# Int8 cross attention: scores read 1024 columns at a time, one weighing per turn, six of eight casts on ScalarE, values held twice

## The reference, cut to what matters

```python
def _fq_sym(x, axis):          # queries, keys, values
    s = jnp.maximum(jnp.max(jnp.abs(x), axis=axis, keepdims=True) / 127.0, 1e-08)
    q = jnp.clip(jnp.round(x / s), -127.0, 127.0) * s
def _fq_unsigned(x, axis):     # probabilities
    s = jnp.maximum(jnp.max(x, axis=axis, keepdims=True) / 255.0, 1e-08)
    q = jnp.clip(jnp.round(x / s), 0.0, 255.0) * s
...
scores = q @ k.T * scale ; p = softmax(scores) ; out = fq_unsigned(p) @ v
```

## Time and profile before

| | |
|---|---|
| median of 3 runs | 2608.09 us (2602.43 to 2608.8) |
| profiled execution | 2601.35 us, span 2599.5 us |
| busy in the span | TensorE 2309.8 us (89%), VectorE 1796.6 (69%), ScalarE 1244.8 (48%), GpSimd 588.7 (23%) |
| int8 stage | from 1522 us to 2139 us of the span |

### The profile page before, as it was taken

How to read it: one execution, slowest core, us unless ns; L and a number is a source line. 1 busy time by engine, 2 the same in 40 slices (tenths; PEclk the granted TensorE clock), 3 DMA queues, 4 the chain that set the end, 5 groups by cost and what they waited for, 6 DMA issues and landing times. The chain is left out here.

```text
span 2599.5 us, 32403 instructions
## 1 busy us (share of the span) xinstructions
PE 2309.8 (89%) x11664; PEld 1576.3 (61%) x11664; DVE 1796.6 (69%) x3528; ACT 1244.8 (48%) x2202; POOL 588.7 (23%) x435
## 2 busy tenths in 40 slices
PE   3779999999999999877897988888888779899998
PEld 2557666666666665555774455545555437677776
DVE  7855777767777779786776976777767763554444
ACT  4443465666565666533443124676767853211111
POOL 7710033333333243430000004222141300000000
PEclk9889999999999999998998999999989879899999
DMA  3331100000000000005444000000000004556662
GB/s 130 114 138 37 37 17 29 9 29 25 13 29 17 29 9 13 1 16 203 162 170 171 0 21 10 1 10 1 10 1 1 21 27 188 188 205 232 234 229 70
DMA packets 47067, 184.89 MB, mean 71 GB/s; under 512 B 6272, under 2 KB 11136, under 8 KB 36672
## 3 DMA queue, kind: packets, MB, share of 16 engines
q1 hardware_dynamic: 46912, 182.86, 19.5%
HBM read 173.93 MB, written 8.91 MB: 70 GB/s over the span
## 5 line engine op out<-in xcount | busy, mean ns | idle before, releaser
L403 PE MATMUL wide_a<-wide_w,ctxT 128*128 128x256 f32 (+1 forms) x2048 | 437.8, 367 | 2.8 <-POOL wide_eps L372 2.8
L403 PEld LDWEIGHTS wide_a<-wide_w,ctxT 128*128 128x128 f32 x2048 | 368.2, 191 | 76.8 <-issue 35.7
L385 POOL TENSOR_TENSOR wide_sums<-wide_sums,wide_s 128x512 f32<-128x512 f32 x224 | 301.9, 1348 | 458.3 <-ACT wide_s L533 445.1
L428 PE MATMUL wide_scores<-wide_q,wide_keysT 128*128 128x512 f32 x512 | 238.4, 604 | 10.8 <-ACT wide_s L529 10.8
L1702 ACT ACTIVATE int_prob<-int_a,int_shift,int_qscale 128x512 uint8<-128x512 f32 x256 | 198.8, 781 | 102.3 <-PE int_a L1551 101.8
L438 PE MATMUL wide_o<-wide_s,wide_values 128*128 128x512 f32 x512 | 232.5, 597 | 3.5 <-ACT wide_s L533 3.5
L529 ACT COPY wide_s<-wide_scores 128x512 f32<-128x512 f32 x256 | 148.5, 586 | 180.0 <-PE wide_scores L428 168.6
L1827 DVE TENSOR_REDUCE int_peaks<-int_a 128x1 f32<-128x512 f32 x256 | 169.3, 684 | 52.9 <-PE int_a L1551 50.9
L1551 PE MATMUL int_a<-int_keys,int_qrows 96*128 96x512 bf16 x512 | 166.5, 408 | 42.6 <-DVE int_peaks L1827 37.3
L428 PEld LDWEIGHTS wide_scores<-wide_q,wide_keysT 128*128 128x128 f32 x512 | 87.9, 189 | 147.0 <-ACT wide_s L529 86.0
L591 DVE TENSOR_TENSOR wide_top<-wide_top,wide_s 128x512 f32<-128x512 f32 x240 | 165.5, 690 | 15.4 <-ACT wide_s L529 9.6
(11 more groups left out here) (426 smaller groups left out, 4283.3 us busy)
## 6 DMA issues: line engine op xcount, KB each, us to landing
moe_gate_up<-hbm_m_gu SPq DMA_DIRECT2D x34, 1408.0 KB, 6.1
moe_down<-hbm_m_down_a SPq DMA_DIRECT2D x34, 512.0 KB, 7.0
causal_wqkv<-hbm_wqkv SPq DMA_DIRECT2D x8, 1536.0 KB, 6.8
ctxT<-hbm_ctxT SPq DMA_DIRECT2D x4, 2048.0 KB, 15.3
oproj_raw<-hbm_wproj SPq DMA_DIRECT2D x8, 1024.0 KB, 5.3
ctxT_again<-hbm_ctxT SPq DMA_DIRECT2D x4, 2048.0 KB, 14.7
moe_down<-hbm_m_down_b SPq DMA_DIRECT2D x34, 192.0 KB, 7.2
wide_unit<-hbm_ffn_units SPq DMA_DIRECT2D x24, 256.0 KB, 2.6
```

The source lines that it names most:

```text
L385: ins = pool.tensor_tensor(sums[0][:, :], before, part[:, j, :], ALU.add)
L403: mm = pe.matmul(a[h][:, j, cols], ctxT[:, kc, t * P:(t + 1) * P], w[g % 2][:, kc, cols], start=(kc == 0), stop=(kc == KC - 1))
L428: pe.matmul(sp_[j % 2][:, :], keysT[:, j, :], q[:, :], start=True, stop=True).then_inc(s_s, 1)
```

## The change

- The four PSUM tiles of 512 columns become two tiles `wide` of 1024 columns. A step `first` or `second` is now two matmuls into one of them, one reduction or one exponential of 1024 columns. `a_free(n)` waits for the reader of tile n-2, so "second" always uses tile 0 and "first" tile 1 (each kind has one tile).
- Order: "first" of a step stands behind the first half of the step's product rather than next to "second". Every turn is followed by one weighing, that of two turns before, across heads too; "summed" (copy of int_sums on VectorE) is a step of its own; "finish" comes two turns after the chunk's last weighing. The four "value turned" are spread over four steps and begin earlier, for which `values` and `pscale` exist twice.
- VectorE casts j = 0 and 4 of a head (in the last chunk j = 0, 2, 4, 6), ScalarE the others; before, VectorE cast the even j (in the last chunk six of eight).
- The program's reserve for DMA descriptors (`dynamic_dma_scratch_size`) goes from 8192 to 2048, which makes room in SBUF.

```diff
-        values = st.sb("values", [P, NCT, P], BF16)
+        values = [st.sb(f"values{i}", [P, NCT, P], BF16) for i in range(2)]
-        a = [st.ps(f"a{i}", [P, 512]) for i in range(4)]
+        wide = [st.ps(f"a{i}", [P, 1024]) for i in range(2)]
+        a = [wide[i // 2][:, i % 2 * 512:(i % 2 + 1) * 512] for i in range(4)]
...
         def cast_on_vector(h, j):
-            if h // HC + 1 == CC:
-                return j % 4 != 3
-            return j % 2 == 0 and not (j % 4 == 2 and h % HC == HC - 1)
+            return j % (2 if h // HC + 1 == CC else 4) == 0
...
                 def a_free(n):
-                    if n >= 4:
-                        who, seen = done_a[n - 4]
+                    if n >= 2:
+                        who, seen = done_a[n - 2]
...
-                    pe.matmul(a[n % 4][:, :], qrows[0:3 * HD, h, t * P:(t + 1) * P],
-                              keys[0:3 * HD, h % HC, j * 512:(j + 1) * 512], start=True, stop=True).then_inc(s_a, 1)
+                    for z in range(2):
+                        j = 2 * p + z
...
+                        mm = pe.matmul(wide[n % 2][:, z * 512:(z + 1) * 512], qrows[0:3 * HD, h, t * P:(t + 1) * P],
+                                       keys[0:3 * HD, h % HC, j * 512:(j + 1) * 512], start=True, stop=True)
+                    mm.then_inc(s_a, 1)
...
-            place(base + 16 + m // 2, "value turned", c, m)
+            place(base + 8 + 3 * m, "value turned", c, m)
...
-        late = [("weigh", h, i) for i in ((j - 2,) if j < ns - 1 else (j - 2, j - 1, j)) if i >= 0]
-        done = [("finish", h // hc, 0)] if j == ns - 1 and h % hc == hc - 1 else []
-        return [("turn", h, j)] + late + done
+    def values_steps(n):
+        steps = [("turn", *divmod(n, ns))] if n < heads * ns else []
+        if n >= 2:
+            h, j = divmod(n - 2, ns)
+            steps.append(("weigh", h, j))
+            if j == ns - 1:
+                steps.append(("summed", h, 0))
+        if n >= hc * ns and n % (hc * ns) == 3:
+            steps.append(("finish", n // (hc * ns) - 1, 0))
+        return steps
...
     for u in range(nu * cc):
-        for j in range(ns):
-            order.append(("second", u, j))
+        for p in range(ns // 2):
+            order.append(("second", u, p))
+            order += at[u * ns + 2 * p]
             if u + 2 < nu * cc:
-                order.append(("first", u + 2, j))
-            order += at[u * ns + j]
-            if u >= 2 and j % 2 == 1:
-                order += values_steps(u // 2 - 1, u % 2 * (ns // 2) + j // 2)
+                order.append(("first", u + 2, p))
+            order += at[u * ns + 2 * p + 1]
+            if u >= 2:
+                order += values_steps((u - 2) * ns // 2 + p)
```

More of the change, by code:

```diff
@@ L1361, in exponentials @@
         def exponentials(h):
-            return done_a[use_a["second", 2 * h + 1, NS - 1]][1]
+            return done_a[use_a["second", 2 * h + 1, NP - 1]][1]
         with nc.Block() as block:
@@ L1540, in score @@
                 def score(step):
-                    what, u, j = step
+                    what, u, p = step
                     n = use_a[step]
@@ L1544, in score @@
                     a_free(n)
-                    if what == "first" and u == 0 and j == 0:
+                    if what == "first" and u == 0 and p == 0:
                         for i in range(2, 4):
@@ L1548, in score @@
                             pe.wait_ge(s_ba if who == "act" else s_bd, seen)
-                    if what == "first" and u % 4 == 0:
-                        pe.wait_ge(s_ba, done_b[use_b["key turned", h // HC, h % HC // 2 * NS + j]][1])
-                    pe.matmul(a[n % 4][:, :], qrows[0:3 * HD, h, t * P:(t + 1) * P],
-                              keys[0:3 * HD, h % HC, j * 512:(j + 1) * 512], start=True, stop=True).then_inc(s_a, 1)
+                    for z in range(2):
+                        j = 2 * p + z
+                        if what == "first" and u % 4 == 0:
+                            pe.wait_ge(s_ba, done_b[use_b["key turned", h // HC, h % HC // 2 * NS + j]][1])
+                        mm = pe.matmul(wide[n % 2][:, z * 512:(z + 1) * 512], qrows[0:3 * HD, h, t * P:(t + 1) * P],
+                                       keys[0:3 * HD, h % HC, j * 512:(j + 1) * 512], start=True, stop=True)
+                    mm.then_inc(s_a, 1)
                 def turn(h, j):
@@ L1691, in keep_turned_values, with exponential @@
                     act.wait_ge(s_b, e + 1)
-                    act.copy(values[:, 8 * m:8 * m + 8, :].rearrange("p a b -> p (a b)"), b[e % 2][:, :]).then_inc(s_ba, 1)
-                def exponential(u, j):
+                    act.copy(values[c % 2][:, 8 * m:8 * m + 8, :].rearrange("p a b -> p (a b)"), b[e % 2][:, :]).then_inc(s_ba, 1)
+                def exponential(u, p):
                     h, t = query(u)
-                    if j == 0:
+                    if p == 0:
                         act.wait_ge(s_pk, u + 1)
@@ L1821, in round_values, with first @@
                     dve.sem_inc(s_vq, 1)
-                def first(u, j):
+                def first(u, p):
                     h, t = query(u)
-                    n = use_a["first", u, j]
+                    n = use_a["first", u, p]
                     dve.wait_ge(s_a, n + 1)
-                    dve.tensor_reduce(peaks[u % 2][:, j:j + 1], a[n % 4][:, :], AX.X, ALU.max).then_inc(s_ad, 1)
-                    if j == NS - 1:
+                    dve.tensor_reduce(peaks[u % 2][:, p:p + 1], wide[n % 2][:, :], AX.X, ALU.max).then_inc(s_ad, 1)
+                    if p == NP - 1:
                         dve.wait_ge(s_ad, done_a[n][1])
@@ L1881, in _ @@
                         keep_turned(x, i)
-                        if i == 0 and x % HC:
-                            keep_sums(x - 1)
+                    elif what == "summed":
+                        keep_sums(x)
                     elif what == "finish":
@@ L2970, in int8_order @@
     order += [("key turned", 0, m * ns + ns - 3) for m in range(2)]
-    order += [("first", u, j) for j in range(ns - 3) for u in range(2)]
+    order += [("first", u, p) for p in range(ns // 2 - 1) for u in range(2)]
     order += [("key middle", 0, ns - 1)]
```

54 lines of the change are left out of this document (28 added, 26 removed).

## The result

| | before | changed |
|---|---|---|
| median | 2605.77 us (4 runs, 2602.43 to 2608.80) | 2578.43 us (4 runs, 2577.38 to 2579.23) |
| span of the profiled execution | 2599.5 us | 2575.9 us |

The ratio is 0.9899, with a 95% interval of 0.9884 to 0.9913: faster by 27 us by the medians, where the forecast was 26. The forecast was built on the profiled execution, and there the drop is smaller: from 2601.35 to 2577.90 us, 23.5.

What follows compares the result with a forecast made beforehand. The prediction took the stage as a lockstep of three nearly level engines, bound by waits between them. Its terms, -10 - 19 + 16 - 6 - 6 - 1 = -26 us, took 2601 to 2575 us; eight in ten: 2545 to 2606.

Steps and rivals of the forecast that it cites:

- Prices: Wide operations of 1024 PSUM columns: a maximum takes 1.22 us until its result, an exponential 1.20 us.
- A, key pairs: Key pairs, set by VectorE: 7.95 us, or 9.10 with its cast, mean 8.52 against 8.93; -10 us over 24 pairs.
- B, weighings: Head ends: the weighings' wait of 1.6 us for the cast goes; 12 heads in chunks 0 to 2, -19 us.
- C, value pairs: Value pairs: "second" waits for the single tile's exponential; 7.41 and 6.74, mean 7.08 against 6.40, +16 us.
- D, turned values and finish: Chunk ends: turned values spread over four steps let copies stand alone; 2 us a chunk, -6 us.
- E, last chunk: Last chunk: VectorE's steps at 4.2 us per two, last units 4.0; 79 against 85.3 us, -6 us.
- The last two units have no maximum: exponential 1.20 + refill 0.70: Last chunk's last two units: this, or + cast 0.90, gives 4.0 us per two steps, 8 steps 16 us.
- F: Tail of 22.3 us: casts in turn on two engines, now four and four; -1 us.
- The front is as before: Chunk 0's own keys and values, ahead of the producing stretches: no change in time.
- The single tile's refill everywhere: Rival: each of 96 steps in chunks 0 to 2 pays a 0.70 us refill; 2626 us; 12%.
- The fall of the clock: Rival: chunks 0 to 2 fall to the last chunk's clock of 0.79; +37 us, 2612; 3%.
- The waits only move: Rival: the weighings' 19 us return as waits for the exponential, key-pair and turned-value gains halve; 2602 us; 11%.

Runs made afterwards that it cites:

- e2: The kernel before with only the two 1024-column tiles and "first" behind the first half of the product; old casts and weighings: 2600.11 us, ratio 0.9993.
- e1: The kernel before with only the new order of turns and weighings, the later finish and doubled values and scales: 2590.15 us, ratio 0.9962.
- e4: The changed kernel with the old weighing distance, three weighings at a head's end and the finish right behind: 2604.94 us, ratio 1.0017.
- e8: The changed kernel with the turned values at their old place, all four in one step: 2581.47 us, ratio 0.9902.
- e6: The changed kernel with casts placed by kind of pair: key pairs on ScalarE, value pairs first on VectorE, second on ScalarE: 2551.58 us, ratio 0.9800.
- e12: The changed kernel with the exponentials of the last two units all on one wide tile: 2583.80 us, ratio 0.9930.
- e3: The changed kernel with its four tiles of 512 columns back, new weighings and casts kept: 2578.50 us, ratio 0.9909.
- e7: The e6 kernel with 512-column reads from four tiles: 2549.44 us, ratio 0.9779.
- e5: The changed kernel with the old split of casts, 66 on VectorE and 62 on ScalarE: 2587.41 us, ratio 0.9926.
- e10: The e6 kernel with the finish of a chunk one turn later: 2550.74 us, ratio 0.9806.
- e9: The e6 kernel with the stage's first four maxima and the turned keys alternating in the written order: 2557.41 us, ratio 0.9823.

## Why the prediction was right, point by point

The side was, and so was the time: 27 us by the medians where the forecast was 26, and 23.5 in the profiled execution, on which it was built. (The prediction says that this execution lay below two of the three runs before; it lay below all three.) The steps that carried the sum fared differently.

**Prices.** Right: 1222 and 1216 ns, against 1.22 and 1.20 us taken.

**A, key pairs, -10.** The loop was right to a hundredth: VectorE over two key pairs of chunk 1, the first without its cast, the second with it.

```profile
1831.37 0.69 DVE L1754 TENSOR_TENSOR int_kf<-int_vp,int_kbias 128x512 f32<-128x512 f32 x1 [1.06 <-PE int_vp L1464]
...
1835.11 1.22 DVE L1830 TENSOR_REDUCE int_peaks<-int_a 128x1 f32<-128x1024 f32 x1
...
1839.31 0.69 DVE L1754 TENSOR_TENSOR int_kf<-int_vp,int_kbias 128x512 f32<-128x512 f32 x1 [1.06 <-PE int_vp L1464]
...
1841.25 1.22 DVE L1852 CAST int_probT<-int_b 128x1024 bf16<-128x1024 uint8 x1
```

7.94 us against 7.95, where the earlier trace rows have 8.93. With VectorE's cast e2 has 9.08 against 9.10; here it is 9.54, since that pair also holds a head's scales. The four key pairs that can be measured alone in each full chunk fell from 37.5 to 34.0 us, 0.87 each, twice the 0.41 of the sum. I took 8.93 for every pair of before; two of the four were 9.89 and 9.72.

**B, weighings, -19.** The mechanism was right (25.8 us of waits to 0.4) and it is the largest term. Its size has no single value: 10 to 13 alone (e1), 26 to 31 within the changed kernel (e4), the finish's place included in both. The 1.6 us of each head weren't paid evenly: before, the pure key pair in which a head ends takes 8.92 us, no more than the one without (8.93), while the value pair in which one ends takes 9.00 and falls to 6.73 in e1.

**C, value pairs, +16.** Right: 7.42 and 6.85 in turn, against 7.41 and 6.74 counted. In the four pure value pairs of a chunk this price eats up what B gives there: they took 9.00, 6.73, 6.40 and 6.40 us before and 7.42, 6.85, 7.42 and 6.85 now, 28.5 both times. TensorE, in the pair before which ScalarE casts first:

```profile
1864.99 0.60 PE L1553 MATMUL int_a<-int_keys,int_qrows 96*128 96x512 bf16 x2 [1.07 <-ACT int_prob L1705]
```

The earlier trace rows have no gap there. It is the named wait, for ScalarE before "second".

**D, turned values and finish, -6.** Not shown. For the values e8 finds nothing clear of the noise. The sign that was named, a unit 3 to 5 us shorter, didn't come: the second unit of a chunk, which held most of the finish before, went from 20.5 to 20.1 us in chunk 1. At its new place the finish costs its unit 1.4 us in the changed kernel (17.1 us in chunk 1 against 15.7 in the same unit of chunk 0, which has no finish) and 3.6 in e6 (18.2 against 14.6), where the sixteen matmuls behind the wait took 3.48 us instead of 2.05.

**E, last chunk, -6.** The term that was off: 11.3. The step of its units with maxima is as counted, 4.18 us from cast to cast against 4.2, with the refill of 0.70 in the open:

```profile
2058.05 1.21 DVE L1852 CAST int_probT<-int_b 128x1024 bf16<-128x1024 uint8 x1
...
2059.18 1.21 DVE L1830 TENSOR_REDUCE int_peaks<-int_a 128x1 f32<-128x1024 f32 x1
...
2061.09 1.23 DVE L1830 TENSOR_REDUCE int_peaks<-int_a 128x1 f32<-128x1024 f32 x1 [0.70 <-PE int_a L1553]
...
2062.23 1.21 DVE L1852 CAST int_probT<-int_b 128x1024 bf16<-128x1024 uint8 x1
```

The six units with maxima took 61.8 us where I had 63 (51, 10 and 2), the last two 12.2 where I had 16. The step of the sum that failed is "The last two units have no maximum: exponential 1.20 + refill 0.70". Without maxima nobody else uses the tiles, so the exponentials alternate between the two and one tile fills while the other is read: two steps took 3.27 us, not 4.0. Putting the refill there (e12) gave 4.09 at full clock, the step as counted, and the two units took 17.3 us, 5.1 more, of which 3.3 are the refill.

Against the kernel before, though, the last two units gave only some 1.6 us (13.8 to 12.2); 9.8 us came from the six with maxima (71.6 to 61.8), where the granted clock rose from 0.79 to 0.97. How much of this is the clock and how much the shorter step, no run separates.

**F and the front.** The tail gave 1.3 for 1. "The front is as before" was wrong by 3 us: the first maxima, now in steps of 1024, stand in the written order behind turned keys, with VectorE idle for 3.64 us. Up to the first exponential the four kernels with tiles of 512 (before, e1, e3, e7) took 83.5 to 83.6 us at a clock of 1.00, the seven others that share the changed kernel's front (e2, e4, e5, e6, e8, e10, e12) 85.2 to 85.7 at 0.98, the changed kernel's own profile 86.5 at 0.96. So some 2 us belong to the wide tiles, and nearly 1 to that execution. That the order is the cause is shown only in part: e9 moved it and got 1.1 us back. The smaller DMA reserve is in all twelve kernels, so no run tests it alone; the stage's DMA share is as before, 0.00 to 0.05 in the chunks.

**The rivals.** The single tile's refill everywhere (2626) did not come; in pairs the other work covered it, and e2 and e3 put the wide reads at nothing. The fall of the clock did not come either: chunks 0 to 2 had 0.98 to 0.99, and the last chunk 0.98 where it had 0.79. Not all of that is the tiles. Like against like, the last chunk had 0.79 with four tiles and 0.96 with two (before, e2), 0.90 and 0.98 (e3, changed), 0.84 and 0.95 (e7, e6). The Trainium skill ("TensorE: Matmul & The Clock Gate", "A second HAM failure mode: psum-queue depth-cycling") tells of a clock lost by cycling through PSUM tiles with short idles between the groups of matmuls. That fewer tiles would make this worse was my own step from there, and these three pairs of traces go the other way. With only one tile in use (e12) the clock stood at 0.82 and then 0.50. "The waits only move" is what e4 is, at 2604.94: without the distance the waits for weighings return, now behind ScalarE's casts. That the forecast held so closely was partly luck: chunks 0 to 2 fell short by 4 and the front by 3, and the last chunk paid 5 of it back.

## What to carry to other kernels

Where several in-order engines run in lockstep, balance the work step by step, not over the whole: find for each kind of step the engine that sets it, and put the movable operation on the other one; nearly the same number of casts on each engine, placed so, was worth another 22 us of the stage. A consumer must stand far enough behind its producer before any work is moved to the producer's engine: here the new split gained nothing without the distance (e4 against e2, which also differ in the turned values), and 7 to 9 us with it (the changed kernel against e5). Merging reads into wider ones saves only the readers' overhead and takes away a tile; where the engines are level, count both sides before doing it.

## What the runs showed of the hardware

A wait of TensorE can cost twice, once as idle time and once by the clock behind it: after 1.66 us of idle time sixteen product matmuls took 3.55 us instead of 1.95 (e1), and with a wait in every step two score matmuls came to 1.03 instead of 0.60 (e12). But it need not: 8.4 us earlier in e1 the same wait was followed by 1.95.

Where such a fall comes isn't fixed by the order of work. Up to the last two units the changed kernel and e12 are the same instructions. The third and the fifth unit of chunk 1, first in the changed kernel, then in e12:

```profile
1782.00:1800.00 18.00, 15.41 (x116) 8.66 (x114) 11.61 (x20) 10.51 (x17) 2.31 (x2) 0.91 0.00 1
1817.10:1835.50 18.40, 16.20 (x154) 13.10 (x154) 15.10 (x27) 13.70 (x21) 4.63 (x4) 1.00 0.00 1
```

```profile
1779.50:1796.20 16.70, 13.90 (x116) 8.21 (x114) 11.84 (x21) 10.44 (x17) 2.31 (x2) 1.00 0.00 1
1813.10:1833.00 19.90, 17.70 (x155) 14.56 (x154) 15.10 (x27) 13.69 (x21) 4.62 (x4) 0.91 0.00 1
```

One execution has the clock at 0.91 in the third unit, the other in the fifth, and from the third to the fifth both take 53.5 us. The third key pair of this chunk is 9.54 us in the changed kernel, 11.03 in e12, 11.04 in e8, 10.95 in e1; in chunk 2 of e8 it is 9.54 again. A difference of 1 to 2 us between single pairs or units of two profiles is therefore no evidence for an edit, e10's first unit included. What decides where the clock falls stays open.
